# Reordering the second attention's loop: PSUM banks, GpSimd queue, place counts, router products

## Time and profile before

| | |
|---|---|
| median of 3 runs | 772.32 us |
| profiled execution | 771.22 us, span 769.4 |
| TensorE / VectorE / ScalarE / GpSimd busy | 85% / 69% / 51% / 40% |
| mean granted TensorE clock | 0.926 |
| second attention's turns 0 to 7 | about 251 to 414 us |
| from there to the first expert tile | to 454.4 us |

### The profile page before, as it was taken

How to read it: one execution, slowest core, us unless ns; L and a number is a source line. 1 busy time by engine, 2 the same in 40 slices (tenths; PEclk the granted TensorE clock), 3 DMA queues, 4 the chain that set the end, 5 groups by cost and what they waited for, 6 DMA issues and landing times.

```text
span 769.4 us, 19214 instructions
## 1 busy us (share of the span) xinstructions
PE 651.1 (85%) x5188; PEld 543.0 (71%) x5189; DVE 528.0 (69%) x1846; ACT 388.7 (51%) x921; POOL 311.3 (40%) x439
## 2 busy tenths in 40 slices
PE   6799999999844889898876329999999999999790
PEld 4679898998723667676655217888888888888340
DVE  2368778878834668787875747777777777777373
ACT  1446565666436566555343614555555555555044
POOL 0246777777550022655668732222222222222132
PEclk9999999999976999989976559999999999999996
DMA  6343443443310000111111322222222222221584
GB/s 202 98 129 100 142 121 101 142 132 83 95 26 16 2 3 2 51 50 58 57 50 68 114 90 65 69 70 81 69 73 78 69 79 73 69 82 56 167 355 154
DMA packets 47709, 68.13 MB, mean 89 GB/s; under 512 B 10576, under 2 KB 34512, under 8 KB 47664
## 3 DMA queue, kind: packets, MB, share of 16 engines
q1 hardware_dynamic: 39080, 46.01, 20.3%
q0 software_dynamic: 6480, 17.87, 6.2%
q10 hardware_dynamic: 2104, 3.68, 1.5%
HBM read 40.21 MB, written 23.12 MB: 82 GB/s over the span
## 4 chain that ended last, share of the span: by engine, by line
PE 33%; issue 28%; DVE 3%; DMA 2%; SPq 1%; ACT 1%; ACTq 0%; DVEq 0%; POOLq 0%
PE half_bank L145 9%; PE half_bank L147 9%; PE half_bank L146 9%; PE half_bank L1920 5%; PE half_bank L1901 2%; DVE region_en_small L155 1%; DMA region_y_rows<-results 1%; DVE region_y_rows L1664 1%; ACT all_w L1678 1%; SPq L1708 1%; DVE all_w L921 1%; DMA results<-all_w_qkv,ex_home 0%; SPq L1707 0%; DVE region_en_small L158 0%; DMA all_xh<-dispatched 0%
## 5 line engine op out<-in xcount | busy, mean ns | idle before, releaser
L1739 POOL DMA_INDIRECT results<-all_w_qkv,ex_home x71 | 68.2, 960 | 201.5 <-DVE all_w_qkv L1864 177.1
L1772 ACT ACTIVATE region_hid_hi<-half_bank 128x256 fp32r<-128x256 f32 x142 | 46.7, 381 | 81.0 <-PE half_bank L1920 81.0
L969 POOL DMA_INDIRECT dispatched<-all_xh,all_slot_u x64 | 67.9, 1062 | 40.2 <-DVE all_slot_u L1341 23.3
L145 PE MATMUL half_bank<-region_w_hi,region_hid_hi 128*128 x284 | 81.4, 287 | 2.5 <-DVE region_hid_lo L1856 2.5
L146 PE MATMUL half_bank<-all_w,region_hid_hi 128*128 x284 | 79.7, 281 | 0.0
L147 PE MATMUL half_bank<-region_w_hi,region_hid_lo 128*128 x284 | 79.5, 280 | 0.0
L1864 DVE TENSOR_SCALAR all_w_qkv<-half_bank,ex_gate 128x256 f32<-128x256 f32 x71 | 34.3, 484 | 49.1 <-PE half_bank L147 48.5
L1759 ACT ACTIVATE all_xh<-half_bank,all_ln_b,all_ln_w 128x128 f32<-128x128 f32 x142 | 57.7, 467 | 18.8 <-PE half_bank L1901 18.8
L145 PE MATMUL half_bank<-region_w_hi,region_x_hi 128*128 x142 | 62.5, 440 | 0.5 <-DVE region_x_lo L1849 0.5
L145 PEld LDWEIGHTS half_bank<-region_w_hi,region_hid_hi 128*128 128x128 f32 x284 | 53.2, 187 | 13.4 <-issue 10.4
L1766 ACT ACTIVATE all_w_proj<-half_bank 128x512 f32<-128x512 f32 x71 | 42.5, 599 | 39.1 <-PE half_bank L147 39.1
(11 more groups left out here) (247 smaller groups left out, 1805.6 us busy)
## 6 DMA issues: line engine op xcount, KB each, us to landing
all_xh<-dispatched SPq DMA_DIRECT2D x71, 130.5 KB
all_w<-in_moe_w_dram SPq DMA_DIRECT2D x32, 256.0 KB, 3.1
region_y_rows<-results SPq DMA_DIRECT2D x12, 512.0 KB, 10.4
all_resid<-at_x SPq DMA_DIRECT2D x32, 128.5 KB
shared_x_t<-in_x_t_dram SPq DMA_DIRECT2D x16, 256.0 KB, 4.2
at_x_tok<-in_x_dram SPq DMA_DIRECT2D x16, 256.0 KB, 4.3
region_y_rows<-results SPq DMA_DIRECT2D x8, 256.0 KB, 9.5
out_dram<-all_w ACTq DMA_DIRECT2D x4, 512.0 KB
```

The lines of the kernel that those rows point to most:

```text
L145: nc.tensor.matmul(out, a_hi, b_hi, start=(start and i == 0), stop=False)
L969: nc.gpsimd.indirect_dma_start(out=dram["dispatched"], out_offset=bass.IndirectOffsetOnAxis(ap=keep["slot_u"][g % SENDS][:, u, k:k + 1], a ...
L1739: nc.gpsimd.indirect_dma_start(out=dram["results"], out_offset=bass.IndirectOffsetOnAxis(ap=home[par][:, 0:1], axis=0), in_=ym[par], in_of ...
L1772: nc.scalar.activation(hid_hi[par][:, cs, :], p_t[half], ACT.Copy).then_inc(s["hid_high"], 1)
```

## The change

- TensorE: `turn_prob(n, 0)` and `turn_prob(n, 1)` now have `turn_rows(n+2, "x")` between them, and `route(n-2)` moves behind them, so that it stands ahead of `outputs(n)`.
- TensorE: `count_places(n-2)` moves from the end of the turn into the middle of `attended(n)`, before its y = 1 half, in all turns but 7.
- VectorE: `route_slots(n-2)` stands before `add(n)` in every turn, not only in turn 7.
- GpSimd: 5 scatters, `residual(n-1)`, 1 scatter, `root(n-1)`, 2 scatters, in place of 6 scatters, `root`, `residual`, 2 scatters. `send_rows` now takes single numbers (tile and choice) so that an odd count can be given.
- Banks: "q" before "kv", and "x" before "p", in the list that gives each entry its bank.

No operation is added or taken out.

```diff
-def send_rows(nc, dram, keep, g, tiles):
+def send_rows(nc, dram, keep, g, numbers):
-    for u in tiles:
-        for k in range(2):
+    for number in numbers:
+        for u, k in (divmod(number, 2),):
...
-        for what, g, parts in (("s", n, 2), ("kv", n + 1, 1), ("q", n + 1, 2), ("p", n, 2), ("x", n + 2, 2), ("o", n, 2),
+        for what, g, parts in (("s", n, 2), ("q", n + 1, 2), ("kv", n + 1, 1), ("x", n + 2, 2), ("p", n, 2), ("o", n, 2),
                                ("v", n + 1, 2), ("a", n, 2), ("h", n - 1, 2)):
...
         for n in range(1, GROUPS):
             if there(n - 3):
-                scatter(n - 3, range(0, 3))
-            root(n - 1)
+                scatter(n - 3, range(0, 5))
             residual(n - 1)
             if there(n - 3):
-                scatter(n - 3, range(3, NI))
-        scatter(GROUPS - 3, range(0, 3))
+                scatter(n - 3, range(5, 6))
+            root(n - 1)
+            if there(n - 3):
+                scatter(n - 3, range(6, 2 * NI))
+        scatter(GROUPS - 3, range(0, 6))
         root(GROUPS - 1)
...
                 route_pick(n - 2)
-                if n == GROUPS - 1:
-                    route_slots(n - 2)
+                route_slots(n - 2)
             if there(n):
                 add(n, 0)
                 add(n, 1)
-            if there(n - 2) and n < GROUPS - 1:
-                route_slots(n - 2)
...
             for y in range(2):
+                if y == 1 and there(g - 2) and g < GROUPS - 1:
+                    count_places(g - 2)
...
             if there(n + 1):
                 project(n + 1)
+            if there(n):
+                turn_prob(n, 0)
+            if there(n + 2):
+                turn_rows(n + 2, "x", s["xh1_ready"], xh1)
+            if there(n):
+                turn_prob(n, 1)
             if there(n - 2):
                 route(n - 2)
-            if there(n):
-                turn_prob(n, 0)
-                turn_prob(n, 1)
-            if there(n + 2):
-                turn_rows(n + 2, "x", s["xh1_ready"], xh1)
...
-            if there(n - 2) and not last:
-                count_places(n - 2)
```

More of the change, by code:

```diff
@@ L1062, in root, with scatter @@
             nc.gpsimd.tensor_scalar(shift_h[:, :], mean[:, :], -1.0, None, ALU.mult).then_inc(s["h_rstd"], 1)
-        def scatter(g, tiles):
+        def scatter(g, numbers):
             wait_apart(pool, s["slots_ready"], g + 1)
-            send_rows(nc, dram, keep, g, tiles)
+            send_rows(nc, dram, keep, g, numbers)
         def residual(g):
@@ L1075, in gpsimd_program @@
             if there(n - 3):
-                scatter(n - 3, range(0, 3))
-            root(n - 1)
+                scatter(n - 3, range(0, 5))
             residual(n - 1)
             if there(n - 3):
-                scatter(n - 3, range(3, NI))
-        scatter(GROUPS - 3, range(0, 3))
+                scatter(n - 3, range(5, 6))
[3 more added lines that the diff above has]
+        scatter(GROUPS - 3, range(0, 6))
         root(GROUPS - 1)
-        scatter(GROUPS - 3, range(3, NI))
-        scatter(GROUPS - 2, range(NI))
-        scatter(GROUPS - 1, range(NI))
+        scatter(GROUPS - 3, range(6, 2 * NI))
+        scatter(GROUPS - 2, range(2 * NI))
+        scatter(GROUPS - 1, range(2 * NI))
         residual(GROUPS - 1)
```

## The result

The changed kernel takes 792.45 us (median of 4 runs, 789.38 to 792.86) beside 772.22 us of the kernel before on the same chip (4 runs, 771.66 to 772.46): a ratio of 1.0254, 95% interval 1.0228 to 1.0281. The forecast was 763.8 us, with 770.0 as the upper end. The profiled execution took 792.86 us, its span is 791.1 us.

What follows compares the result with a forecast made beforehand. TensorE was taken to set the pace, with gaps. Turns 3 to 6 -10.6, turn 0 -1.1, late signals +1.0 and turn 7 +2.2 gave -8.5 us: 763.8 us, range 759.5 to 770.

Steps and rivals of the forecast that it cites:

- `route_slots` before the adds: VectorE: its 1.62 us fills the wait for `attended`, so the probabilities' chain starts about 0.2 after `project`, not 1.03.
- The residual on GpSimd: Moved off VectorE's pick, freeing 1.82 us; holds the second probability multiplication 0 to 1.15 us a turn.
- Late signals: ScalarE's copy of the probabilities before `outputs`, 2.2 us late on average; +1.0 taken, from nothing to four times 2.2.
- The arithmetic of the turn: Turns 3 to 6: 18.3 us if TensorE never waits, 19.3 if VectorE is held fully; 19.0 taken.
- Place counts: Five tiny matmuls in the middle of `attended` wait 0 to 0.6 us for `picked`; 0 taken.
- Its rival: Counts in `attended` stall the projection if the pick stays held: +4.1 us, 776.4 us; chance 0.12.
- Banks: Turn 0: `outputs` no longer waits 1.12 us for VectorE's `values`, since its bank comes from "q"; -1.1 us.
- Turn 7: Without `project`, the moved router products stand between transposes and `outputs`: cost +1.0 to +2.6 us, +2.2 taken.

Runs made afterwards that it cites:

- after_third: The changed kernel, unchanged, on a chip where the kernel before takes about 762 us: 765.98 us, ratio 1.0071.
- before_again: The kernel before, unchanged, profiled again on the 772 chip: 770.86 us (one run).
- gated: The changed kernel with GpSimd's first five scatters of a turn held until the score products fill their last bank, on a 762 chip: 757.32 us, ratio 0.9942.
- pool_only: The kernel before with only GpSimd's new order (five scatters, residual, one, root, two): 761.54 us, ratio 0.9991.
- pe_banks: The kernel before with only TensorE's new order of transposes and router products and the new bank list: 762.80 us, ratio 1.001.
- slots_only: The kernel before with only `route_slots` ahead of the adds and the counts in the middle of `attended`: 769.05 us, ratio 1.0099.
- gated_again: The gated kernel, unchanged, on the 772 chip: 766.77 us, ratio 0.9933.

## Why the prediction was wrong

**"`route_slots` before the adds" together with "The residual on GpSimd" is the step that failed.** The prediction wrote that slots made earlier let the first scatter start "some 3 to 4 us earlier, P - 2", and then asked only where the residual would land. It never asked what the scatters themselves land on. P - 2 is just ahead of the 64 score products, and five scatters then lie beside all of them; the start itself was forecast rightly (P - 2.3 in after_third). The cost of that neighbour stood at nothing, without a reason. The runs show in its place +2.5, +5.3, +5.2, +5.2 and +6.2 us of pauses in the scores of turns 3 to 7, and +1.3 to +2.7 in `project`, most of it from the lower clock. In turns 3 to 6 that makes 25.8 us of the 26.55 that they took above 4 x 18.3. These turns make most of the 29 us between forecast and result: against 4 x 19.0, turns 3 to 6 took 99.75, which is 23.8 more, and turn 7 with what follows took 5.9 more than its +2.2.

**"Late signals" held the warning.** The 2.2 us that L1157 stood for a "remote" releaser while GpSimd issued scatters was read as a delay of a signal, and was taken at +1.0 because five of the six scatters would be over by then. "Up to four times 2.2 if it stops TensorE itself" stood there as an end; the pauses were more than twice that in turns 4 to 7. The late signals and the pauses share the scatters, and they share the chip: the kernel before has 10.8 and, in before_again, 10.6 us of waits for a remote releaser in L1157 on the 772 chip, and every trace from there has some such wait in turns 3 to 7 or just behind them. None of the seven traces from the 762 chips has one. That both have one cause is likely, and not shown.

**The arithmetic of the turn held where nothing is paused.** gated on a 762 chip has turns of 18.8 and one of 19.2 (forecast 19.0), `outputs` directly behind the products, the pick unheld, L1267 0.12 after `project`. That the number is so close is in part luck: nothing is held there, so the forecast's own figure for the case is 18.3. `outputs` starts 9.3 after P for 9.6, and the rest takes 9.6 for 8.7, of which 0.39 is the wait for the place counts. The kernel before has no trace on a 762 chip; judged by pool_only (78.2) and pe_banks (79.7), which both take its time, its turns 3 to 6 take some 78 to 80 us there and not 86.6. So there is less to gain: 4.7 us measured, and not 10.

**"The residual on GpSimd"**: bound 0 to 1.15, measured 1.35 to 1.70 in after_third. The mechanism was right and the size too low; the operation held is the first multiplication and not, as forecast, the second, because the five scatters start 1.26 apart and not 1.4, and the residual comes at P + 3.7 and not P + 5. With the hold, turns take 20.2 to 21.2 on that chip, where the forecast had 19.3 at most. So the change without a gate misses its forecast there too, by the sign: 1.0071 of the kernel before.

**"Place counts"**: 0.50 and 0.44 us of waiting in turns 2 and 6 of the changed kernel, 0.39 to 0.75 in turns 2 to 6 of gated, inside the 0 to 0.6 of the forecast or little above, but in nearly every turn, where the sum had nothing. Its rival needed a held pick, and slots_only has that: 2.02 us.

**"Banks"**: turn 0 went from 17.3 to 16.2, as forecast. Ahead of the loop the profiled execution was 1.5 us longer; the start of turn 0 lies anywhere from 250.0 to 255.5 us in the sixteen traces, so one pair of traces can't tell a change there.

**"Turn 7"**: in the changed kernel the products take 3.42 us between transposes and `outputs`, near the forecast's price, yet in gated_again the stretch from turn 7's scores to the first expert is 450.16 - 389.68 = 60.5 us, for 61.7 before and 63.1 in before_again. That stretch holds the wait for the gather, which differs between traces by more than the term looked for: 5.4 us from the last scatter's end in gated_again, 6.9 in the first trace, 9.7 in before_again. Up to the last scatter's end it is 55.1 us in gated_again, for 54.8 and 53.3. So +0.3 to +1.8 of the +2.2 is there, by single traces, and its size stays open. Of the +8.1 in the changed kernel, 6.2 are the pauses of its scores (406.86 to 414.2, less 1.16).

What stays open: why the handfuls come 0.7 us apart, whether the number or the size of the matmuls counts, whether the loading of TensorE's own instructions has a part in it, why one chip does it and two don't, and whether a plain GpSimd DMA would do it as well as an indirect one. The runs show where the pauses are and what moves them, not what in the chip makes them.

## What to carry to other kernels

When a step lets GpSimd's scatters start earlier, look at what TensorE and VectorE will be issuing beside them, and not only at what waits for them: a burst of many small matmuls is the place to keep clear, and a group of large ones did better in these runs, though not without late signals. One wait on a bank that is filled anyway is enough to steer them. Parts that are neutral or worse alone can gain together, and a loss can have two causes on two chips, so a version is worth running on more than one. A delay that the profile can't name should be carried into the sum at its full size for every new neighbour that its suspected cause gets.

## What the runs showed of the hardware

- With GpSimd's indirect DMAs beside them, 64x64 matmuls were issued in handfuls (mostly of 4) about 0.72 us apart on the 772 chip, after 30 to 50 that went through; 64 took 3.6 to 7.4 us for 1.16. The 48 large matmuls of `project` kept 5.40 us beside the same scatters when they came first (gated_again), and paused by 0.30 and 0.60 us when the small ones came first (turn 3 of the changed kernel).
- On the 772 chip ScalarE and VectorE also waited near the scatters for TensorE's work that by its rows was done: 10.8 us in 5 waits in the kernel before, 7.1 us in 3 with the gate. No trace of a 762 chip has such a wait.
- The same program on a 762 chip, with the same overlap: no pause, nor in slots_only on the other one. The kernel before is 10 us apart between the chips as well (about 762 and 772).
- A GpSimd addition of 128x512 stretched a VectorE multiplication of two SBUF inputs from 0.69 us to between 2.04 and 2.39.
- A plain DMA costs GpSimd about 0.55 us to issue (five in 2.78, twelve in 6.48), an indirect one 0.96 and 0.30 between two.
